# Scores of two heads at a time, then both masks, and one maximum over two PSUM banks

## The reference

```
x = x + attn(layernorm(x))          # 16 heads of 16 channels, q and k normalised per head
x = x + block(layernorm(x))         # inside: rmsnorm, 16-head latent attention, rmsnorm, 8 experts + 1 shared

# both attentions, for each sequence and each of the 16 heads:
s = q @ k.T                         # 512 x 512, the second one divided by sqrt(64)
s = where(tril, s, -1e30 or -inf)   # causal mask
p = softmax(s)                      # exp(s - max(s)) / sum
o = p @ v
```

## Time and profile before

| what | value |
|---|---|
| median of 3 runs | 4112.76 us |
| lowest and highest run | 4105.27, 4118.48 us |
| span of the profiled execution, first to last instruction | 4099.4 us |
| PE matmul busy | 3512.7 us, 86% |
| DVE busy | 3056.1 us, 75% |
| ACT busy | 2303.1 us, 56% |
| L1049, the maxima, DVE | 2048 instructions, 884.5 us |
| L833, the exponentials, ACT | 2048 instructions, 1060.8 us |
| L608, the masks, PE | 2048 instructions, 450.4 us |

### The profile page before, as it was taken

One profiled execution on the slowest core, in us unless ns is written; L12 is line 12 of the kernel. 1 busy time (PEld: TensorE's weight loads), 2 busy tenths in 40 slices (PEclk: granted clock), 3 DMA queues, 4 the chain that ended last, 5 costly groups with the idle time before them and its releaser, 6 DMA issues.

```text
span 4099.4 us, 93010 instructions
## 1 busy us (share of the span) xinstructions
PE 3512.7 (86%) x31392; PEld 2772.0 (68%) x31392; DVE 3056.1 (75%) x6444; ACT 2303.1 (56%) x6346; POOL 776.0 (19%) x919
## 2 busy tenths in 40 slices
PE   3898988989889898898988889888898988989888
PEld 2676766767667676676766767666676766767667
DVE  3878777787777877768787787877778777787776
ACT  2656546565465664646655465654656546565464
POOL 1212222022120221212122121222202212022120
PEclk9999999999899999999999999998999989999899
DMA  3000000000000000000000000000000000000000
GB/s 73 7 2 7 7 7 7 2 7 7 7 7 1 8 6 7 7 7 7 2 7 7 7 7 2 7 7 7 7 2 7 7 7 7 2 7 7 6 1 6
DMA packets 33906, 30.35 MB, mean 7 GB/s; under 512 B 8864, under 2 KB 33312, under 8 KB 33376
## 3 DMA queue, kind: packets, MB, share of 16 engines
q1 hardware_dynamic: 33376, 23.68, 2.0%
HBM read 15.28 MB, written 8.39 MB: 6 GB/s over the span
## 4 chain that ended last, share of the span: by engine, by line
PE 56%; issue 14%; DVE 13%; ACT 10%; POOL 5%; SPq 1%; ACTq 0%; DMA 0%; DVEq 0%; POOLq 0%
PE bank L619 12%; PE scores L717 9%; ACT prob L833 6%; PE bank L630 6%; PE scores L606 6%; PE bank L729 5%; PE scores L607 4%; PE scores L608 3%; POOL qf L499 2%; PE scores L691 2%; PE scores L671 2%; PE scores L602 2%; PE bank L590 2%; DVE negmax L1049 1%; DVE stk L1145 1%
## 5 line engine op out<-in xcount | busy, mean ns | idle before, releaser
L833 ACT ACTIVATE prob<-scores,negmax 128x128 f32<-128x128 f32 (+3 forms) x2048 | 1060.8, 538 | 223.6 <-DVE negmax L1049 180.2
L1049 DVE TENSOR_REDUCE negmax<-scores 128x1 f32<-128x128 f32 (+3 forms) x2048 | 884.5, 483 | 102.0 <-PE scores L608 88.4
L619 PE MATMUL bank<-ident,prob 128*128 128x128 f32 x5120 | 731.2, 280 | 44.5 <-DVE probt L1057 35.1
L1057 DVE COPY probt<-bank 128x512 f32<-128x512 f32 x896 | 596.6, 683 | 180.1 <-PE bank L619 173.1
L619 PEld LDWEIGHTS bank<-ident,prob 128*128 128x128 f32 x5120 | 548.6, 142 | 155.5 <-DVE probt L1057 65.9
L606 PE MATMUL scores<-khh,qt 128*128 128x256 f32 (+2 forms) x1024 | 439.2, 430 | 13.3 <-issue 6.6
L608 PE MATMUL scores<-mask,ident 128*128 128x128 bf16 x2048 | 450.4, 231 | 0.0
L833 ACT ACTIVATION_READ_ACCUMULATOR prob<-scores,negmax 128x1 f32 x2048 | 438.0, 214 | 0.0
L804 ACT ACTIVATE probt<-bank 128x512 f32<-128x512 f32 x384 | 233.0, 607 | 205.3 <-PE bank L619 205.3
L607 PE MATMUL scores<-kll,qt 128*128 128x256 f32 (+2 forms) x1024 | 346.1, 338 | 0.0
L590 PE MATMUL bank<-ident,stk 128*96 128x128 bf16 x2048 | 206.9, 288 | 149.8 <-DVE stk L1147 119.7
(11 more groups left out here) (178 smaller groups left out, 6937.0 us busy)
## 6 DMA issues: line engine op xcount, KB each, us to landing
x_in<-in_x_rows SPq DMA_DIRECT2D x16, 512.0 KB, 3.5
out_rows<-x SPq DMA_DIRECT2D x16, 512.0 KB, 3.5
r_gu<-in_wg SPq DMA_DIRECT2D x2, 512.0 KB, 5.1
r_gu<-in_wu SPq DMA_DIRECT2D x2, 512.0 KB, 5.1
r_d<-in_wd SPq DMA_DIRECT2D x1, 1024.0 KB, 6.5
r_wqt<-in_wq_nope_t SPq DMA_DIRECT2D x1, 512.0 KB, 6.8
r_wqr<-in_wq SPq DMA_DIRECT2D x2, 256.0 KB, 8.6
r_wob<-in_wo SPq DMA_DIRECT2D x1, 512.0 KB, 5.3
```

The lines of the kernel that those rows point to most:

```text
L619: ins = nc.tensor.transpose(bank[4 + n % 2][:, q * P:(q + 1) * P], prob[:, u % 2, q, i * P:(i + 1) * P], ident[:, :])
L833: nc.scalar.activation(prob[:, u % 2, q, 0:n], bank[q][:, 0:n], ACT.Exp, bias=negmax[:, a, u, q:q + 1], accum_out=sums[:, a, u, q:q + 1]). ...
L1049: nc.vector.tensor_reduce(negmax[:, a, u, M * part:M * part + M], scores[:, M * part:M * part + M, 0:n], axis=AX.X, op=ALU.max, negate=Tru ...
L1057: nc.vector.tensor_copy(probt[:, u % 2, i], bank[4 + n % 2][:, :]).then_inc(probt_dve.sem, 1)
```

## The change: two heads per step

M becomes 2, so NM becomes 2. PE writes the scores of heads 0 and 1, then both masks, and raises `s_psum` once; the same for heads 2 and 3. DVE takes the maximum of two banks in one instruction. ACT still runs one exp per head, but waits for a maximum once per two heads.

```
-M = 1
+M = 2
...
-            for q in range(M * part, M * part + M):
+            heads = range(M * part, M * part + M)
+            for q in heads:
                 h = g * G + q
                 if u > 0:
                     pe.wait_ge(prob_ready.sem, prob_ready.at(b, (a * UNITS + u - 1) * G + q + 1))
...
                     mm(bank[q][:, 0:m], tok, khh[:, 0:m], start=True, stop=False)
                     mm(bank[q][:, 0:m], tok, kll[:, 0:m], start=False, stop=False)
+            for q in heads:
                 ins = mm(bank[q][:, n - P:n], ident16[:, :], mask16[:, :], start=False, stop=True)
             ins.then_inc(s_psum.sem, 1)
```

## The result

The changed kernel took 4155.91 us (median of 4 runs, 4150.17 to 4159.21), the kernel before beside it 4113.32 us (4 runs, 4105.27 to 4118.48). The ratio is 1.0103, 95% interval 1.0089 to 1.0117: slower by 1.0%. The forecast was 4150, between 4107 and 4184.

A forecast was written before the change was run, and what follows sets the result against it. It took the first attention as bound by a loop through several engines, the second by PE. Span 4099.4 + 46 (first) - 9 (second) = 4136.4, plus 13.4 from span to median, gave 4150 us; own range 4128 to 4172, with rivals 4107 to 4184.

The forecast's parts named there:

- The maximum itself: On DVE, a two-bank maximum costs its columns: 0.68, 0.95 and 1.21 us for two heads of 256, 384, 512.
- The bound below: On DVE, the low limit for a two-bank maximum: no longer than one bank's, 0.55 us for 384 columns.
- The first attention, middle groups: Loop in the first attention: 0.17 later at j = 1, 0.40 at j = 2, 0.06 from masks, sum 0.63 us per group.
- The first group of the first attention: Start of the first attention: 1.0 us longer, from waiting for two heads' exps, the longer maximum and the mask.
- The second attention: PE's queue there: -0.52 + 0.34 = -0.18 us per group, 0.54 us saved per sequence, in all -9 us.
- The gap before block 5: Second attention, j = 3: PE's block 5 transpose waits for DVE's copy of block 3, at s + 4.30, 0.34 us later.
- The gain of PE's order: Second attention: weight loads hide better, saving 0.16, 0.16 and 0.20 us at j = 0, 1, 2, in all 0.52 a group.
- The last group: End of the second attention: transposes wait about 0.5 us longer with no scores behind, so it gains nothing.
- The sum: Whole kernel: span 4099.4 + 46 - 9 = 4136.4, plus 13.4 by which the median exceeded the span: 4150 us.
- Rival 1: Block 5 wait does not matter; the second attention's PE gain (46 us) pays back the first: 4113 us, chance 0.18.
- Rival 2: No gain from PE's matmul order; a second attention group is 0.44 us longer: 4187 us in all, chance 0.15.
- Rival 3: DVE's queue decides, at copies behind the maxima; 67 us saved, 4046 us in all, chance 0.10.

The follow-up runs named there:

- e9: Kernel before, with the two-bank maximum only at j = 1 and 2 of the first attention and j = 0, 1, 2 of the second: 4130.39 us, ratio 1.0084.
- e10: Kernel before, with the two-bank maximum only at j = 0 and 3 of the first attention and j = 3 of the second: 4131.31 us, ratio 1.0089.
- e3: Kernel before, with both masks behind two heads in both attentions, one raise and one maximum per head kept: 4128.56 us, ratio 1.0061.
- e4: Kernel before, with one raise and one two-bank maximum per two heads in both attentions, PE's order kept: 4196.70 us, ratio 1.0222.
- e11: e8 with `onm` late in the second attention too and `osb` behind all four exps of j = 1: 4041.51 us, ratio 0.9871 to the kernel before.
- e8: Kernel before, with `onm` late in the first attention, masks paired in the second, block 3 copied before the last maximum of j = 3 in both: 4055.77 us.
- e5: Kernel before, with `onm` moved behind the four maxima of j = 2 in both attentions: 4079.93 us, ratio 0.9931.
- e6: Changed kernel, with `onm` moved behind the maxima of j = 2 in both attentions: 4156.61 us, ratio 1.0130 to the kernel before.
- e2: Kernel before, with the whole change in the second attention only: 4119.82 us, ratio 1.0045.

## Why the prediction was right, and where it was not

- *The maximum itself.* Right: 0.69, 0.95 and 1.22 us, two steps as long as their columns. The bound below, one bank's time, was far off.
- *The first attention, middle groups.* Right in mechanism, place and size: 13.83 against 13.88, by 0.16 until `osb` of j = 1 and 0.40 at j = 2. e9 and e10 show that it is these two units, e3 and e4 that it is the maximum: the masks' order adds next to nothing here. The three distances between the `onm` of an attention are 14.06, 13.83 and 12.94 us for 13.25, 13.25 and 12.55 before: +0.81, +0.58 and +0.39, together 1.78 where I had 3 x 0.63 = 1.89.
- *The first group of the first attention.* Too small. From the first score to the first `onm` it is 17.55 instead of 16.04, +1.5 where I had 1.0, and there the masks' order counts for 0.6 of it (e3). With it an attention is 3.3 us longer, not 2.9, which makes 53 us. The rest of the 57 goes with the clock: in 6 of 16 sequences this start took 18.5 to 18.7 us, and in exactly these the granted clock of the stretch was 0.81 to 0.91 instead of 1.00. In the trace of before it was 3 of 16, with 0.89 and 16.7 us.
- *The second attention.* This term was wrong, even in its sign. The gap before block 5 was right: s + 4.34 for s + 4.30, so +0.38 for +0.34. The gain of PE's order was over-sized. From the first score of a unit to what PE does behind the four heads it saves 0.12, 0.13 and 0.06 us at j = 0, 1 and 2, in all 0.31 where I had 0.52. So a middle group is +0.07 for a forecast of -0.18. Over all four units the experiments say the same: the order gives 0.46 (e4 against the changed kernel) where I had 0.52 + 0.10, and the maximum costs 0.51 to 0.53 (e4, e10) where I had 0.44. At j = 2 I had missed that PE, now earlier, runs into the exp of head 3 of the unit before, which ACT does after `osb`: the second L607 of the last pair is 0.42 us long where that of the first pair is 0.34 (rows 1255.47 and 1254.60 above). In e11, where `osb` is out of its way, both are 0.34, and a group wins 0.09 over e8 (`onm` is late there as well, but that alone left 15.12 in e5).
- *Its ends, and luck.* The last group, for which I had nothing in balance, lost 0.49 (12.88 to 13.37), and the start, for which I had no price of its own, 0.4 (20.4 to 20.8 us to the first `onm`, at a granted clock of 0.92 in both traces). At this clock a whole second attention takes 63.7 us for 62.7, +1.0 where I had -0.54; over 16 sequences that would be +16 us for -9. The sums of the two traces differ by only +2 because in the trace of before 9 of 16 starts had a granted clock of 0.85 and cost some 1.4 us more (rows in the last section), while in the changed kernel none was below 0.90. All seven traces in which the second attention has its masks in pairs are free of such starts, the other six have between 1 and 11 each; whether the order keeps the clock up or this is chance, no run settles.
- *The sum.* I had added +46 - 9 = 37 to the median of before. The medians moved by 43, the two traces by 55. The 13.4 us that I took for what lies around the span was mostly something else: around the changed kernel's it is 1.9 (4156.72 to 4154.8), so the traced execution of before was some 11.5 us quicker than its median. Against the traces, two terms were too small by 11 each, the rest came out 4 shorter than I had it, and the 13.4 was 11.5 too large: the total is closer than its parts deserve.
- *Rival 1*, that both effects cancel, fell with the changed kernel's gap of 0.33 before block 5 and its group of 15.18, longer than before and not 0.7 shorter. *Rival 2* fell with e4 against the changed kernel, 15.65 to 15.19. *Rival 3*, DVE's queue as the bound, fell as told: DVE is 61 us less busy and nothing is faster. But its germ was true, since a copy behind maxima in that queue is what PE waits for, and e5 and e8 gain by changing the order in the queue (e8 also PE's order) rather than its work.
- ACT waits 0.85 instead of 0.44 us for its exp of j = 2. The Trainium skill, "Perfetto Trace Analysis", section "Optimizing Scalar/DVE Operations", says that where VectorE is not saturated but causes bubbles on other engines, breaking up instructions may let work finish sooner. The trace agrees, from the other side: DVE was busy for 11.77 of 13.25 us, and with merged instructions the work finishes later.

## What to carry to other kernels

Merging two instructions saved their fixed part (0.065 us a step) and delayed the first result by the whole second half (0.27 to 0.53 us) plus the wait for its input. Ask first whether the engine is the bound or only a station in a loop; in a loop the second price is paid in every turn. What helps there is the order in the queue: what nobody waits for goes behind what somebody does (e5, e8). With long instructions in the queue even that can only move the wait (e6).

## What the runs showed of the hardware

The stretch between the two attentions, the same code in all kernels, took between 39 and 42 us in every trace; in that of before 39.2 us in 8 of 16 sequences, 40.9 in 3 and 41.7 in 5 (to 0.3 us). Granted clock is the column before the last two. A long case and a short one, both in the trace of before:

```profile
679.00:682.00 3.00, 0.00 (x0) 0.00 (x0) 1.75 (x10) 0.00 (x0) 1.34 (x2) 0.83 0.49 156
682.00:685.00 3.00, 1.97 (x8) 1.54 (x8) 2.78 (x9) 1.02 (x2) 0.81 (x1) 0.50 0.06 19
685.00:688.00 3.00, 2.89 (x7) 2.25 (x8) 0.89 (x2) 0.06 (x1) 0.00 (x0) 0.50 0.00 0
688.00:691.00 3.00, 3.00 (x9) 2.06 (x8) 0.82 (x3) 0.75 (x2) 0.73 (x1) 0.50 0.00 0
691.00:694.00 3.00, 2.71 (x12) 1.85 (x10) 1.21 (x4) 1.14 (x3) 0.31 (x1) 0.96 0.00 0
```

```profile
1184.00:1187.00 3.00, 0.00 (x0) 0.00 (x0) 1.75 (x11) 0.00 (x0) 1.49 (x2) 0.86 0.49 168
1187.00:1190.00 3.00, 2.00 (x9) 1.57 (x9) 2.79 (x8) 1.08 (x2) 0.67 (x1) 0.50 0.02 6
1190.00:1193.00 3.00, 3.00 (x7) 2.34 (x8) 0.75 (x2) 0.07 (x1) 0.00 (x0) 0.50 0.00 0
1193.00:1196.00 3.00, 3.00 (x14) 2.32 (x13) 0.82 (x3) 1.12 (x3) 0.74 (x1) 1.00 0.00 0
```

PE does nothing for over 3 us while the norm is computed, the clock falls to 1.2 GHz (0.50), and with the same work behind it stays there for two of these 3 us slices in one sequence and for three in another. Over a run the stretch sums to 635 to 657 us in the traces here, which is more than several of the effects under study. It is 9.5 of the 14 us by which e2's trace is longer than that of before, and it is why small changes are better read from the distance between two like events than from the total.

The starts of the attentions vary in the same way. From the first score of the second attention to its first `onm`, two sequences of before and one of the changed kernel:

```profile
1217.08:1238.93 21.85, 21.85 (x202) 17.45 (x202) 15.10 (x33) 14.15 (x49) 0.61 (x1) 0.85 0.01 1
2718.76:2739.13 20.37, 20.37 (x202) 16.16 (x202) 14.92 (x33) 13.81 (x49) 0.61 (x1) 0.92 0.01 2
...
216.71:237.51 20.80, 20.38 (x202) 16.56 (x203) 13.72 (x22) 13.49 (x49) 0.61 (x1) 0.92 0.00 1
```

And of the first attention of the changed kernel, a long start and a usual one:

```profile
1134.09:1152.82 18.73, 16.42 (x180) 11.61 (x180) 13.63 (x22) 13.26 (x49) 0.61 (x1) 0.91 0.00 1
372.63:390.18 17.55, 15.45 (x180) 10.66 (x180) 13.57 (x21) 13.15 (x49) 0.61 (x1) 1.00 0.00 1
```

The weight load of float32 data in front of a matmul hides under a 512-column matmul of float32 data and not under the 128-column mask: 0.47 against 0.40 us for the same L607, by what stands ahead of it. A pair of heads saved 0.08 to 0.09 us by it with 512 columns and some 0.06 with 256.
